# Graph network kernel: the last stages' messages all scattered by GpSimd, none summed by TensorE

## Chip, cores and metric

One NeuronCore of one Trainium2 chip runs the whole program. The metric is the device time of one execution in microseconds; lower is better. Engines: TensorE (PE) multiplies matrices, VectorE (DVE) and ScalarE (ACT) work element by element, GpSimd (POOL) here almost only issues indirect DMAs (gathers and scatters of rows), SyncE (SP) issues the plain DMAs.

## What is computed

A graph of N = 12,500 nodes with D = 16 features and E = 400,000 edges (`src`, `dst`, sorted by `dst`). Four blocks follow each other, each with a residual and a layer norm:

```python
x = layernorm(x + L0(x))   # two graph attention layers
x = layernorm(x + L1(x))   # two graph convolutions
x = layernorm(x + L2(x))   # sheaf: per edge two Householder reflections
x = layernorm(x + L3(x))   # tensor product of node features and edge attributes
# sheaf (L2)
deg = zeros.at[src].add(1).at[dst].add(1)
out = x - zeros.at[src].add(msg_s) - zeros.at[dst].add(msg_d)
# product (L3)
m   = silu(einsum('ei,ej,ijh->eh', x[dst], edge_attr, W) * norm)
agg = segment_sum(m @ W_lin, src)
```

What matters here is the sum of per-edge messages **by source node**. Edges are sorted by destination, so sums by `dst` are scans along the edges; sums by `src` need another way.

## The kernel before

Edge number e = lane * 3125 + column: each of the 128 partitions ("lanes") holds 3,125 consecutive edges. They are worked through in NCH = 25 chunks of CH = 125 columns, and within a chunk in groups of GRP = 5 columns (NG = 25 groups), with two buffers per tile (`b` is 0 or 1).

Two ways to sum by source stand side by side, split by column. The first DC = 20 columns of each chunk (DG = 4 groups) are **direct**: class `DirectSums` (L1310) adds their messages to a PSUM accumulator of all nodes. Per column VectorE makes two one-hot tiles of the source number (L1349, L1351) and their wide product with the message, 128 x 1600 (L1354), and TensorE multiplies that in (four products of 400 columns, L1339). The other SC = 105 columns (SG = 21 groups) are **scattered**: GpSimd writes each column's 128 rows to their places in source order in a DRAM table, one indirect DMA per column (`scatter_column_loop`, L1152). Afterwards `src_order_scan` reads that table in order and scans it, chunk by chunk (16 scans of 105 columns per chunk, L1724), and `extract` picks up the ends.

The place of an edge in source order is its `rank`. It is made along the way: `histograms` counts nodes (beside the first attention gather), `count_in_group` counts equal sources within a group (beside the second attention gather), and `count_before_group` looks up and advances a running table, one group at a time. The last is split over the two graph convolutions: the first (stage names c1...) takes 11 groups of each chunk, the second (c2...) 10.

The order of the work around the change is written by hand, one loop per engine with semaphores between:

- `gcn_gather` (c1 and c2): GpSimd gathers the first 85 columns of each chunk (L494). VectorE and TensorE find the other 40 by matching (`Match`: L1269 makes 13 tiles per step, ten steps a chunk), and each round of VectorE's loop also does one group of `count_before_group` (L1097 to L1108: two one-hot tiles, a lookup tile, a wait for TensorE, a product, a reduction, an add). The loop has as many rounds as the longer of the two: `for m in range(max(NB + 1, side.groups))`, NB + 1 = 11. After it come 16 scans (L975).
- `sheaf_edges` (se...): GpSimd's queue is gather(i+1), scatter(i), gather(i+2), scatter(i+1) and so on: 125 gathers and 105 scatters per chunk. VectorE, TensorE and ScalarE work on chunk i group by group, and the direct columns of chunk i-1 are put between its groups 0 to 19.
- `product_edges` (pe...): GpSimd only scatters, five columns at a time as ScalarE finishes a group (L1851). Per group VectorE makes an outer product (L1787), TensorE transposes (L1815), ScalarE copies (L1849), TensorE multiplies (L1822), ScalarE applies silu. The chunk's own direct columns begin after its first four groups.

```python
for t in range(SC):
    ...
    g.indirect_dma_start(out=view, in_=M[b][:, DC + t, :], in_offset=None,
                         out_offset=bass.IndirectOffsetOnAxis(ap=stage[b][:, t:t + 1], axis=0)
                         ).then_inc(sent[b], 16)
```

## Time and profile before

| | us |
|---|---|
| median of 3 runs | 32684.31 |
| lowest and highest | 32668.05, 32695.04 |
| the profiled execution, its own time | 32672.44 |
| its span, first to last instruction | 32670.6 |
| second attention gather (g2g), first to last gather | 6160.7 to 10135.7 |
| first gcn gather (c1c) | 11322.2 to 14729.9 |
| second gcn gather (c2c) | 15144.2 to 18560.0 |
| sheaf edges, first gather to last scatter | 18959.2 to 27201.0 |
| product edges, first to last scatter | 27984.8 to 32009.8 |

The profile records each instruction of one execution. "Busy" counts the time in an instruction; waits are given by what ended them. A DMA issued by GpSimd is a POOL instruction whose length is the time that POOL spends on issuing it, not the transfer. Line numbers are those of the kernel before.

### The profile page before, as it was taken

Reading aid. Unit: us, or ns where it says so; the run is one execution under the profiler, and the core shown is the slowest. Engines: PE = TensorE matmul, PEld = TensorE weight load, DVE = VectorE, ACT = ScalarE, POOL = GpSimd, SP = SyncE. Lnnn points to the kernel's source line nnn. Section 1 sums busy time; section 2 is a strip of 40 time slices with the busy share of each in tenths; the row PEclk is TensorE's granted clock in tenths of the full one; section 3 lists DMA queues with packets and bytes.
Section 4 is the critical chain, followed back from the end, with each engine's and each line's share of the span. In section 5 each row is a group of like instructions: output and inputs, shape, how many; then the busy total and the mean of one; then the engine's idle time right before and its main releaser. Section 6 shows DMA issues by size and latency. Waiting matters only on the chain. (4 is left out here: it accounts for less than half of the span.)

```text
span 32670.6 us, 266258 instructions
## 1 busy us (share of the span) xinstructions
PE 13491.3 (41%) x71326; PEld 10479.5 (32%) x71326; DVE 16103.5 (49%) x34560; ACT 2584.3 (8%) x3901; POOL 22511.4 (69%) x20275
## 2 busy tenths in 40 slices
PE   1111100211110177775777535444444441666663
PEld 1111100211110166664666423232323230454442
DVE  3434429344443677775777534444444443444442
ACT  0000000000000000000000001011111110333330
POOL 5777760477775288885888767777777774777772
PEclk5555555555555588886888756666666665777775
DMA  2111113111112311111111110000000002000001
GB/s 55 16 15 16 16 10 145 22 27 27 27 27 46 111 33 33 33 32 21 33 33 33 25 15 12 14 12 14 12 14 12 14 10 59 18 15 15 15 13 56
DMA packets 1117655, 946.20 MB, mean 29 GB/s; under 512 B 609084, under 2 KB 1060308, under 8 KB 1092308
## 3 DMA queue, kind: packets, MB, share of 16 engines
q1 hardware_dynamic: 468516, 706.27, 7.3%
q0 software_dynamic: 646368, 201.76, 6.4%
q10 hardware_dynamic: 1872, 28.29, 0.2%
q8 instruction: 307, 5.03, 0.1%
q14 instruction: 592, 4.85, 0.1%
HBM read 506.74 MB, written 428.17 MB: 29 GB/s over the span
## 5 line engine op out<-in xcount | busy, mean ns | idle before, releaser
L494 POOL DMA_INDIRECT g1g_G<-tab,g1g_stage x3125 | 3270.3, 1046 | 1237.8 <-issue 1025.7
L494 POOL DMA_INDIRECT se_G<-tab,se_stage x3125 | 3324.5, 1064 | 1085.3 <-issue 1072.5
L494 POOL DMA_INDIRECT g2g_G<-tab,g2g_stage x3125 | 2949.5, 944 | 1272.5 <-issue 1026.4
L1152 POOL DMA_INDIRECT messages<-pe_M,pe_rstage x2625 | 3178.9, 1211 | 905.3 <-issue 817.5
L1152 POOL DMA_INDIRECT messages<-se_M,se_rstage x2625 | 2980.1, 1135 | 865.7 <-issue 799.6
L494 POOL DMA_INDIRECT c2c_G<-tab16b,c2c_stage x2125 | 2769.4, 1303 | 856.0 <-issue 647.3
L494 POOL DMA_INDIRECT c1c_G<-tab,c1c_stage x2125 | 2761.3, 1299 | 793.7 <-issue 647.3
L1053 DVE SCALAR_TENSOR_TENSOR g2gh_junk<-g2gh_pB,g2gh_src_f,earlier 128x128 f32<-128x128 f32 (+4 forms) x2625 | 1453.7, 614 | 1951.3 <-POOLq L493 1928.0
L1567 PE MATMUL se_pTV<-ident,se_pair 128*32 128x128 f32 x3125 | 539.5, 313 | 4159.9 <-DVE se_pair L1474 4159.4
L739 PE MATMUL g1gh_acc<-g1gh_oh_hi,g1gh_oh_lo 128*128 128x100 bf16 x6250 | 539.0, 283 | 3746.7 <-DVE g1gh_oh_hi L719 3746.7
L1065 PE MATMUL g2gh_pB<-ident_b,src_lo 128*128 128x128 bf16 x2625 | 641.4, 286 | 3290.3 <-DVEq L1059 3249.5
L1278 PE MATMUL c1cm_acc<-c1cm_hot,c1cm_part 128*128 128x512 f32 x6500 | 1740.7, 429 | 344.3 <-DVE c1cm_hot L1269 344.3
L1278 PE MATMUL c2cm_acc<-c2cm_hot,c2cm_part 128*128 128x512 f32 x6500 | 1717.2, 425 | 400.9 <-DVE c2cm_hot L1269 400.9
L1567 PEld LDWEIGHTS se_pTV<-ident,se_pair 128*32 128x32 f32 x3125 | 283.8, 106 | 4534.9 <-issue 4486.2
L739 PEld LDWEIGHTS g1gh_acc<-g1gh_oh_hi,g1gh_oh_lo 128*128 128x128 bf16 x6250 | 508.6, 143 | 3777.1 <-DVE g1gh_oh_hi L719 3777.1
L717 DVE TENSOR_TENSOR g1gh_oh_lo<-dst_lo,iota 128x640 bf16<-128x640 f32 (+1 forms) x625 | 514.6, 823 | 2284.6 <-POOLq L493 2231.8
L1473 DVE COPY se_pair<-se_G 128x80 f32 (+1 forms) x625 | 139.9, 224 | 2888.7 <-DMA se_G<-tab,se_stage 2761.6
L1278 PEld LDWEIGHTS c1cm_acc<-c1cm_hot,c1cm_part 128*128 128x128 f32 x6500 | 1356.2, 213 | 640.7 <-issue 336.7
L1278 PEld LDWEIGHTS c2cm_acc<-c2cm_hot,c2cm_part 128*128 128x128 f32 x6500 | 1338.2, 210 | 691.3 <-issue 389.2
L1787 DVE TENSOR_TENSOR pe_outer<-pe_X,pe_A 128x640 f32 x625 | 520.9, 833 | 1941.8 <-PE pe_pT L1815 1855.5
L1065 PEld LDWEIGHTS g2gh_pB<-ident_b,src_lo 128*128 (+1 forms) x2625 | 278.4, 106 | 3433.3 <-issue 3187.5
L1822 PE MATMUL pe_pM<-p_wm,pe_outT 128*128 128x16 f32 x6250 | 905.2, 283 | 1034.6 <-ACT pe_outT L1849 1034.6
(607 smaller groups left out, 34105.5 us busy)
## 6 DMA issues: line engine op xcount, KB each, us to landing
scans<-g1w_W SPq DMA_DIRECT2D x25, 3187.5 KB, 10.0
c1cm_row<-match SPq DMA_DIRECT2D x500, 128.0 KB, 3.0
c2cm_row<-match SPq DMA_DIRECT2D x500, 128.0 KB, 3.0
edges<-g2g_G SPq DMA_DIRECT2D x25, 2062.5 KB, 6.8
g2w_G<-edges SPq DMA_DIRECT2D x25, 2062.5 KB, 11.6
scans<-g2w_W SPq DMA_DIRECT2D x25, 2062.5 KB, 7.3
g1g_G<-tab,g1g_stage POOLq DMA_INDIRECT x3125, 2.4
g2g_G<-tab,g2g_stage POOLq DMA_INDIRECT x3125
```

The lines of the kernel that those rows point to most:

```text
L494: g.indirect_dma_start(out=G[b][:, t, :], out_offset=None, in_=table, in_offset=bass.IndirectOffsetOnAxis(ap=stage[b][:, t:t + 1], axis=0) ...
L717: v.tensor_tensor(oh_lo[o][b][:, part, :], bc(lo[:, at], [P, m, P], 2), bc(k.iota[:, :], [P, m, P], 1), ALU.is_equal).then_inc(ready, 1)
L739: mm = pe.matmul(acc[2 if o and direct else o][:, 0:NT], oh_lo[o][b][:, g, :], oh_hi[o][b][:, g, :], start=False, stop=True, skip_group_ch ...
L1053: ins = v.scalar_tensor_tensor(out=junk[g][:, :], in0=pB[b][:, a * GRP * P:(e + 1) * P], scalar=src_f[:, e:e + 1], in1=k.earlier[:, (GRP - ...
L1065: pe.matmul(pB[b][:, e * P:(e + 1) * P], k.src_lo[:, at].to_broadcast([P, P]), k.ident_b[:, :], start=True, stop=False)
L1152: g.indirect_dma_start(out=view, in_=M[b][:, DC + t, :], in_offset=None, out_offset=bass.IndirectOffsetOnAxis(ap=stage[b][:, t:t + 1], axis=0)
L1278: mm = pe.matmul(self.acc[m % 2][:, :], self.part[part][:, j * MR:(j + 1) * MR, :].rearrange("p r f -> p (r f)"), self.hot[m % 2][:, j, :] ...
L1473: ch(v.tensor_copy(pair[:, :, 0, :], G[b][:, at, 0:D]))
L1567: mm = pe.transpose(pT[:, g * P:(g + 1) * P], pair[:, g, :, :].rearrange("p n d -> p (n d)"), k.ident[:, :])
L1787: v.tensor_tensor(outer[:, :, :, :], bc(X[b][:, at, :], [P, GRP, D, DE], 3), bc(A[b][:, at, :], [P, GRP, D, DE], 2), ALU.mult).then_inc(ou ...
L1822: mm = pe.matmul(pM[:, g * D:(g + 1) * D], outT[:, g * P:(g + 1) * P], w[:, :], start=True, stop=True)
```

## The change

The direct sums go: class `DirectSums` and all its calls in both stages, the third histogram, and the blocks that add its result. All 125 columns of a chunk are scattered. So the rank is needed for 25 groups instead of 21: `count_in_group` does 25, `count_before_group` 13 in the first graph convolution and 12 in the second. The tables in source order have 3,125 places per lane instead of 2,625, and `src_order_scan` scans 125 columns per chunk.

```diff
@@ -33,11 +33,6 @@
 PAIRS = NCH // 2
 GRP = 5
 NG = CH // GRP
-DG = 4
-DC = DG * GRP
-SG = NG - DG
-SC = SG * GRP
-LS = NCH * SC
 NT = 100
 NP = NT * P
 XT = 25
...
-    steps = [(at, min(size, DC - at), True) for at in range(0, DC, size)] + [(at, min(size, CH - at), False) for at in range(DC, CH, size)]
-    return steps, max(n for _, n, _ in steps)
+    steps = [(at, min(size, CH - at)) for at in range(0, CH, size)]
+    return steps, max(n for _, n in steps)


 def histograms(k, c, name):

...
-    steps = -(-SG // per)
+    steps = -(-NG // per)
     pB = [c.ps(f"{name}_pB{b}", [P, 2048]) for b in range(2)]
     junk = [c.sb(f"{name}_junk{g}", [P, (g + 1) * P]) for g in range(GRP)]
...
@@ -1144,12 +1139,12 @@
 def scatter_column_loop(g, i, j, b, view, M, stage, staged, ready, sent, parts=1):

     g.wait_ge(staged[b], (j + 1) * 16)
-    for t in range(SC):
+    for t in range(CH):
         if parts == 1 and t == 0 or parts > 1 and t % GRP == 0:

-            g.wait_ge(ready, i + 1 if parts == 1 else i * NG + (DG + t // GRP + 1))
+            g.wait_ge(ready, i + 1 if parts == 1 else i * NG + (t // GRP + 1))
             g.nop(nofuse=True)
-        g.indirect_dma_start(out=view, in_=M[b][:, DC + t, :], in_offset=None,
+        g.indirect_dma_start(out=view, in_=M[b][:, t, :], in_offset=None,
                              out_offset=bass.IndirectOffsetOnAxis(ap=stage[b][:, t:t + 1], axis=0)
                              ).then_inc(sent[b], 16)

...
-                s.dma_start(k.rank_lanes.rearrange("p (i c) -> p i c", c=CH)[:, :, DC:CH],
-                            k.rank[:, :].rearrange("p (i c) -> p i c", c=CH)[:, :, DC:CH]).then_inc(stored, 16)
+                s.dma_start(k.rank_lanes, k.rank[:, :]).then_inc(stored, 16)
                 s.wait_ge(stored, 16)

...
@@ -1307,71 +1301,13 @@
                       self.out[:, at:at + BE * D].rearrange("p (e f) -> p e f", f=D)).then_inc(self.emptied, 1)


-class DirectSums:
...
-    def tensor_first(self, pe):
-        pe.wait_ge(self.hot, 4)
-        for b in range(2):
-            self.products(pe, b, b == 0)
-
-    def products(self, pe, b, start):
-        for q in range(self.BANKS):
-            mm = pe.matmul(self.acc[:, q, 0:self.w * D], self.oh_lo[b][:, :],
-                           self.wide[b][:, q * self.w:(q + 1) * self.w, :].rearrange("p t d -> p (t d)"),
-                           start=start, stop=True, skip_group_check=True)
-        mm.then_inc(self.added, 1)
-
-    def vector(self, v, k, M, i, d, b):
-
-        m = i * DC + d
-        at = bass.ds(i * CH + d, 1)
-        v.wait_ge(self.added, m + 1)
-        v.tensor_tensor(self.oh_lo[b][:, :], k.iota[:, :], k.src_lo[:, at].to_broadcast([P, P]),
-                        ALU.is_equal).then_inc(self.made, 1)
-        v.tensor_tensor(self.oh_hi[b][:, :], k.iota[:, 0:NT], k.src_hi[:, at].to_broadcast([P, NT]),
-                        ALU.is_equal).then_inc(self.hot, 1)
-        v.wait_ge(self.hot, m + 5)
-        v.tensor_tensor(self.wide[b][:, :, :], bc(self.oh_hi[b][:, :], [P, NT, D], 2),
-                        M[:, bass.ds(d, 1), 0:D].to_broadcast([P, NT, D]), ALU.mult).then_inc(self.made, 1)
-
-    def tensor(self, pe, i, d, b):
-        pe.wait_ge(self.made, (i * DC + d) * 2 + 2)
-        self.products(pe, b, False)
-
-    def vector_last(self, v, out):
-        v.wait_ge(self.added, NCH * DC + 2)
-        for q in range(self.BANKS):
-            v.tensor_copy(out[:, q * self.w:(q + 1) * self.w, :],
-                          self.acc[:, q, 0:self.w * D].rearrange("p (t d) -> p t d", d=D)).then_inc(self.out_sem, 1)
-
-
 def release_messages(g, b, j, sent, mfree):

-    g.wait_ge(sent[b], (j + 1) * (16 * SC))
+    g.wait_ge(sent[b], (j + 1) * (16 * CH))
...
-                            sums.vector(v, k, M[1 - b], i - 1, d, half)
-
...
-                    spread_column(0, 0)
                     evacuate(0)
-                    with v.Fori(0, DC // 2 - 1) as m:
-                        ch.enter(m, 10)
-                        group_step(2 * m + 1, 1)
-                        group_step(2 * m + 2, 0)
-                        ch.leave(DC // 2 - 1, 10)
-                    group_step(DC - 1, 1)
-                    with v.Fori(DC, NG - 1) as q:
-                        ch.enter(q - DC, 5)
+                    with v.Fori(1, NG - 1) as q:
+                        ch.enter(q - 1, 5)
                         group_step(q)
-                        ch.leave(NG - 1 - DC, 5)
+                        ch.leave(NG - 2, 5)
                     v.wait_ge(evacuated, i * NG + (NG - 1))
                     group_dots(NG - 2)
...
                 with v.Fori(0, PAIRS) as j:
                     ch.enter(j, 2 * per)
-                    chunk(2 * j + 1, 1, j, True)
-                    chunk(2 * j + 2, 0, j + 1, True)
+                    chunk(2 * j + 1, 1, j)
+                    chunk(2 * j + 2, 0, j + 1)
                     ch.leave(PAIRS, 2 * per)
-                v.nop(nofuse=True)
-                with v.Fori(0, DC // 2) as m:
-                    sums.vector(v, k, M[0], NCH - 1, 2 * m, 0)
-                    sums.vector(v, k, M[0], NCH - 1, 2 * m + 1, 1)
-                sums.vector_last(v, direct)

             @block.tensor
             def _(pe):
-                def chunk(i, direct_before):
+                def chunk(i):

                     def transpose(n):
...
-                    with pe.Fori(0, DC // 2) as m:
-                        for half in range(2):
-                            group_step(2 * m + (1 + half), 2 * m + half if direct_before else None, half)
-                    with pe.Fori(DC + 1, NG - 1) as q:
+                    with pe.Fori(1, NG - 1) as q:
                         group_step(q)
                     hidden_layer(i * NG + (NG - 1))
                     pe.wait_ge(evacuated, i * NG + (NG - 1))
                     vectors(i * NG + (NG - 1))
-                sums.tensor_first(pe)
-                chunk(0, False)
-                with pe.Fori(0, PAIRS) as j:
-                    chunk(2 * j + 1, True)
-                    chunk(2 * j + 2, True)
-                with pe.Fori(0, DC // 2) as m:
-                    sums.tensor(pe, NCH - 1, 2 * m, 0)
-                    sums.tensor(pe, NCH - 1, 2 * m + 1, 1)
+                over_chunks(pe, lambda i, b, j: chunk(i))

             @block.scalar
...
@@ -1787,23 +1689,11 @@
                         v.tensor_tensor(outer[:, :, :, :], bc(X[b][:, at, :], [P, GRP, D, DE], 3),
                                         bc(A[b][:, at, :], [P, GRP, D, DE], 2), ALU.mult).then_inc(outered, 1)
                     v.nop(nofuse=True)
-                    with v.Fori(0, DG + 1) as q:
+                    with v.Fori(0, NG) as q:
                         outer_products(q)
-                    v.wait_ge(silued, i * NG + DG)
-                    v.nop(nofuse=True)
-                    with v.Fori(0, DC // 2) as m:
-                        outer_products(2 * m + (DG + 1))
-                        sums.vector(v, k, M[b], i, 2 * m, 0)
-                        outer_products(2 * m + (DG + 2))
-                        sums.vector(v, k, M[b], i, 2 * m + 1, 1)
-                    v.wait_ge(sums.made, (i + 1) * (2 * DC))
                     v.wait_ge(outered, (i + 1) * NG)
-                    v.sem_inc(dfree, 1)
                     v.sem_inc(used, 1)
-                v.sem_inc(dfree, 2)
-                sums.vector_first(v)
                 over_chunks(v, chunk, ch, 2 + D + 1)
-                sums.vector_last(v, direct)

             @block.tensor
...
+                    with pe.Fori(0, NG) as q:
                         transpose(i * NG + q)
                         multiply(i * NG + q)
-
-                    with pe.Fori(0, DC // 2) as m:
-                        for half in range(2):
-                            n = i * NG + 2 * m + (DG + 1 + half)
-                            transpose(n)
-                            sums.tensor(pe, i, 2 * m + half, half)
-                            multiply(n)
-                sums.tensor_first(pe)
                 over_chunks(pe, chunk)

             @block.scalar
             def _(a):
                 def chunk(i, b, j):
...
@@ -2174,16 +2055,16 @@
                 ch(v.tensor_tensor(agg[:, :, :], agg[:, :, :], bc(dinv[:, :], [P, NT, D], 2), ALU.mult))
             vector_block(k, name + "f", finish)

-        half = SG // 2 + 1
+        half = NG // 2 + 1
         aggregate("c1", k.x[:, :, :], tab16, lambda k, c, n: count_before_group(
-            k, c, n, DG, half, k.by_src["start"]))
+            k, c, n, 0, half, k.by_src["start"]))
         with ExitStack() as s2:
             h = Ctx(nc, s2).sb("c_h", [P, NT, HG])
             node_linear(k, "ch", agg, w1[:, :], h, D, HG)
             batch_norm_relu(k, "cn", h, b1, gamma, beta, HG)
             node_linear(k, "co", h, w2[:, :], y, HG, D)
         aggregate("c2", y[:, :, :], tab16b, lambda k, c, n: count_before_group(
-            k, c, n, DG + half, SG - half, k.free_place))
+            k, c, n, half, NG - half, k.free_place))

         def residual(v, ch):
             ch(v.tensor_tensor(y[:, :, :], agg[:, :, :], bc(b2[:, :], [P, NT, D], 1), ALU.add))
...
         vector_block(k, "sd", degrees)
         root_inverse(k, "sr", xd[:, :, D], xd[:, :, D], 1e-5)
         store_nodes(k, "st", [xd[:, :, :]], tab)
```

Two places where the instruction streams differ, as they stand in program order. `ISA` rows are waits and no-ops, `REGISTER_ALU` rows compute addresses and counts. First VectorE at the end of a chunk of the first gcn stage (`c1ch_...` are the tiles of `count_before_group`, `c1cm_...` those of the matching). Before:

```order
L1102 TENSOR_SCALAR c1ch_loT<-c1ch_pB,part 128x640
L1105 TENSOR_TENSOR c1ch_prod<-c1ch_pR,c1ch_oh_hi 128x500
L75 REGISTER_ALU
L1107 TENSOR_REDUCE c1ch_r<-c1ch_prod 128x5
L75 REGISTER_ALU
L1108 ISA
L1108 TENSOR_TENSOR rank<-c1ch_r,rank 128x5
L1306 COPY c1c_G<-c1cm_out 128x64
L972 ISA
L973 REGISTER_ALU
L975 ISA
L975 SCALAR_TENSOR_TENSOR c1c_G<-keep_d,carry,c1c_G 128x125 x16
```

The eleventh round's group, the last copy of matched columns, then the scans. In the changed kernel two more groups stand between that copy and the scans. The first begins so:

```order
L1103 TENSOR_TENSOR rank<-c1ch_r,rank 128x5
L1300 COPY c1c_G<-c1cm_out 128x64
L1091 REGISTER_ALU
L1092 ISA
L1092 TENSOR_TENSOR c1ch_oh_lo<-src_lo,iota 128x640
L1094 REGISTER_ALU
L1094 TENSOR_TENSOR c1ch_oh_hi<-src_hi,iota 128x500
```

and the second ends so:

```order
L1100 TENSOR_TENSOR c1ch_prod<-c1ch_pR,c1ch_oh_hi 128x500
L70 REGISTER_ALU
L1102 TENSOR_REDUCE c1ch_r<-c1ch_prod 128x5
L70 REGISTER_ALU
L1103 ISA
L1103 TENSOR_TENSOR rank<-c1ch_r,rank 128x5
L967 ISA
L968 REGISTER_ALU
L970 REGISTER_ALU
L970 SCALAR_TENSOR_TENSOR c1c_G<-keep_d,carry,c1c_G 128x125 x16
```

These two groups have no matching step beside them. The second place is VectorE in the product stage, from the sixth group of a chunk on. Before:

```order
L1794 ISA
L1787 ISA
L1787 REGISTER_ALU
L1787 TENSOR_TENSOR pe_outer<-pe_X,pe_A 128x640
L1348 ISA
L1349 ISA
L1349 TENSOR_TENSOR ped_ohl<-iota,src_lo 128x128
L1351 REGISTER_ALU
L1351 TENSOR_TENSOR ped_ohh<-iota,src_hi 128x100
L1353 REGISTER_ALU
L1354 ISA
L1354 TENSOR_TENSOR y<-ped_ohh,pe_M 128x1600
```

After each outer product (L1787) the one-hot tiles and the wide product of a direct column follow. In the changed kernel the loop over the groups has the outer product alone, and the next chunk follows:

```order
L1692 UNCONDITIONAL_BRANCH
L1692 ISA
L1689 ISA
L1689 REGISTER_ALU
L1689 TENSOR_TENSOR pe_outer<-pe_X,pe_A 128x640
L1692 REGISTER_ALU
L1692 COMPARE_AND_BRANCH
L1694 ISA
L1682 ISA
L1682 TENSOR_SCALAR pe_begin<-keep_d 128x125
```

On GpSimd the order is the same, with 125 in place of 105 scatters in a row.

## Rows read from the trace of the kernel before

**Rows 1.** the page: busy time by engine, and POOL in 40 slices

```profile
PE 13491.3 (41%) x71326; PEld 10479.5 (32%) x71326; DVE 16103.5 (49%) x34560; ACT 2584.3 (8%) x3901; POOL 22511.4 (69%) x20275
...
POOL 5777760477775288885888767777777774777772
```

**Rows 2.** groups by line: xcount | busy us, mean ns | idle before, its releasers

```profile
L494 POOL DMA_INDIRECT se_G<-tab,se_stage x3125 | 3324.5, 1064 | 1085.3 <-issue 1072.5 <-DMA se_stage<-in_src_dram 12.8
...
L1152 POOL DMA_INDIRECT messages<-pe_M,pe_rstage x2625 | 3178.9, 1211 | 905.3 <-issue 817.5 <-ACT pe_M L1851 64.8 <-DMA messages<-pe_M,pe_rstage 23.0
L1152 POOL DMA_INDIRECT messages<-se_M,se_rstage x2625 | 2980.1, 1135 | 865.7 <-issue 799.6 <-DVE se_M L1533 66.1
L494 POOL DMA_INDIRECT g2g_G<-tab,g2g_stage x3125 | 2949.5, 944 | 1272.5 <-issue 1026.4 <-DMA g2g_stage<-in_src_dram 246.1
...
L1349 DVE TENSOR_TENSOR sed_ohl<-iota,src_lo 128x128 f32<-128x128 f32 x500 | 146.3, 293 | 125.4 <-DVE se_dots L1487 116.4 <-PE sed_acc L1339 8.4 <-DVE carry L1544 0.5
```

**Rows 3.** waits: engine line <- what ended them: us in total, times, longest us

```profile
DVE se_pair L1473 <- DMA se_G<-tab,se_stage: 2761.6, 24, 150.3
...
DVE g2gh_junk L1053 <- POOLq L493: 1928.0, 398, 21.6
...
ACT L1849 <- POOLq L1371: 509.6, 10, 53.2
...
POOL messages L1152 <- ACT pe_M L1851: 64.8, 17, 58.2
```

**Rows 4.** instructions by tile, carry: ns min/median/max, first and last start us

```profile
L978 DVE COPY carry<-c1c_G x25: 174/176/383, 11467.5 to 14778.6; 128x16 f32<-128x16 f32 x25
L978 DVE COPY carry<-c2c_G x25: 174/175/386, 15294.6 to 18568.4; 128x16 f32<-128x16 f32 x25
...
  DMA c2c_G<-tab16b,c2c_stage: 119.3, 24
...
  DMA c1c_G<-tab,c1c_stage: 6.4, 1
```

**Rows 5.** instructions by tile, se_M: ns min/median/max, first and last start us

```profile
L1152 POOL DMA_INDIRECT messages<-se_M,se_rstage x2625: 954/959/2592, 19313.7 to 27201.0; - x188
```

**Rows 6.** timeline, sheaf stage, 20404 to 20407: start us, us, engine, line

```profile
20403.70 1.83 DVE L1354 TENSOR_TENSOR s_agg<-sed_ohh,se_M 128x1600 f32<-128x1600 f32 x1 [0.16 <-DVE sed_ohh L1351]
...
20404.50 1.86 POOL L1152 DMA_INDIRECT messages<-se_M,se_rstage  x1 [0.30 <-issue]
```

**Rows 7.** busy by window: us, PE, PEld, DVE, ACT, POOL busy (x), PEclk, DMA

```profile
19140.00:19260.00 120.00, 105.92 (x341) 70.73 (x341) 31.20 (x123) 26.74 (x36) 90.75 (x97) 0.50 0.10 7
19500.00:19560.00 60.00, 0.00 (x0) 0.00 (x0) 52.00 (x62) 0.00 (x0) 49.03 (x37) 0.50 0.17 42
19680.00:19780.00 100.00, 97.67 (x441) 64.28 (x439) 65.33 (x161) 23.74 (x34) 79.47 (x68) 0.95 0.05 6
```

**Rows 8.** timeline, product stage, 28107 to 28109

```profile
28107.43 0.83 DVE L1787 TENSOR_TENSOR pe_outer<-pe_X,pe_A 128x640 f32 x1 [3.43 <-PE pe_pT L1815]
28107.67 1.42 POOL L1152 DMA_INDIRECT messages<-pe_M,pe_rstage  x1 [0.30 <-issue]
```

**Rows 9.** timeline, first gcn stage, VectorE at the end of a chunk

```profile
12142.36 0.68 DVE L1105 TENSOR_TENSOR c1ch_prod<-c1ch_pR,c1ch_oh_hi 128x500 f32<-128x500 f32 x1 [4.57 <-PE c1ch_pR L1127]
...
12144.91 0.84 DVE L1097 TENSOR_TENSOR c1ch_oh_lo<-src_lo,iota 128x640 bf16<-128x640 f32 x1
...
12149.81 0.68 DVE L1105 TENSOR_TENSOR c1ch_prod<-c1ch_pR,c1ch_oh_hi 128x500 f32<-128x500 f32 x1 [2.54 <-PE c1ch_pR L1127]
...
12151.53 0.22 DVE L1306 COPY c1c_G<-c1cm_out 128x64 f32<-128x64 f32 x1
12151.88 6.03 DVE L975 TENSOR_TENSOR_SCAN c1c_G<-keep_d,carry,c1c_G 128x125 f32<-128x125 f32 x16
```

**Rows 10.** timeline, second gcn stage, VectorE in the last round of a chunk

```profile
16381.16 0.23 DVE L1306 COPY c2c_G<-c2cm_out 128x64 f32<-128x64 f32 x1 [1.16 <-PE c2cm_out L1298]
```

**Rows 11.** timeline, product stage's scan, one chunk

```profile
32068.91 5.36 DVE L1724 TENSOR_TENSOR_SCAN ps_O<-keep_s,carry,ps_G 128x105 f32<-128x105 f32 x16
```

More of the change, by code:

```diff
@@ L708, in vector @@
     def vector(v, ch, i, q, b, landed):
-        start, n, _ = steps[q]
+        start, n = steps[q]
         v.wait_ge(used, i * len(steps) + q + 1)
@@ L734, in tensor @@
     def tensor(pe, i, q, b):
-        start, n, direct = steps[q]
+        _, n = steps[q]
         pe.wait_ge(ready, i * made[-1] + made[q])
@@ L1368, in release_messages, with sheaf_edges @@
 def release_messages(g, b, j, sent, mfree):
-    g.wait_ge(sent[b], (j + 1) * (16 * SC))
+    g.wait_ge(sent[b], (j + 1) * (16 * CH))
     g.nop(nofuse=True).then_inc(mfree[b], 1)
-def sheaf_edges(k, name, table, scans, messages, first, carry, w1, b1, w2, b2, direct, wide):
+def sheaf_edges(k, name, table, scans, messages, first, carry, w1, b1, w2, b2):
     F = D + 1
@@ L1400, in sheaf_edges @@
         pH = c.ps(name + "_pH", [P, 2, 512])
-        sums = DirectSums(c, name + "d", wide)
         staged = [c.sem(f"{name}_staged{b}") for b in range(2)]
@@ L1731, in _, with product_edges @@
                     v.tensor_reduce(k.whole[:, :], k.keep_s[:, :], axis=AX.X, op=ALU.min).then_inc(whole, 1)
-def product_edges(k, name, attr, messages, first, w, direct, wide):
+def product_edges(k, name, attr, messages, first, w):
     with ExitStack() as st:
@@ L1746, in product_edges @@
         pM = c.ps(name + "_pM", [P, 512])
-        sums = DirectSums(c, name + "d", wide)
         rstaged = [c.sem(f"{name}_rstaged{b}") for b in range(2)]
@@ L2291, in residual @@
             ch(v.tensor_tensor(y[:, :, :], y[:, :, :], agg[:, :, :], ALU.add))
-            ch(v.tensor_tensor(y[:, :, :], y[:, :, :], direct[:, :, :], ALU.add))
             ch(v.tensor_tensor(y[:, :, :], y[:, :, :], bc(xd[:, :, D], [P, NT, D], 2), ALU.mult))
@@ L2312, in product @@
         agg = c.sb("p_agg", [P, NT, D])
-        direct = c.sb("p_direct", [P, NT, D])
         load_small(k, "pl", [
@@ L2320, in product @@
         spread(k, "pp", k.x, D, tab, first[:, 0:D])
-        product_edges(k, "pe", attr, messages, first, wm, direct, (y, agg))
+        product_edges(k, "pe", attr, messages, first, wm)
         src_order_scan(k, "ps", messages, scan16, carry, D, False)
@@ L2324, in product @@
         extract(k, "px", scan16, k.by_src, y, D, ALU.add)
-        vector_block(k, "pj", lambda v, ch: ch(v.tensor_tensor(y[:, :, :], y[:, :, :], direct[:, :, :], ALU.add)))
         node_linear(k, "pn", y, wl[:, :], agg, D, D)
```

111 lines of the change are left out of this document (42 added, 69 removed).

## The prediction

> **What bounds the kernel now.** I start with the page: POOL is the busiest engine, 69% of the span and 5 to 8 tenths in nearly every slice, and the stages where it is not are short [rows 1]. The groups by line say with what: indirect DMAs, each about 1 us busy with 0.3 us of "issue" ahead of it, and almost nothing waited for [rows 2]. In the sheaf stage 5,750 of them take 3324.5 + 1085.3 + 2980.1 + 865.7 = 8256 us, which is the length of the stage (18959.2 to 27201.0). In the product stage 2,625 take 3178.9 + 905.3 = 4084 us, again the stage. So both are bound by POOL's queue. The waits show the others idle behind it: VectorE waits 2761.6 us for gathered rows in the sheaf stage (115 us per chunk), ScalarE 509.6 us for POOL to free a buffer in the product stage, VectorE 1928 us for POOL in the second attention gather [rows 3].
>
> The two gcn stages are different. In c1 VectorE ends a chunk every (14778.6 - 11467.5) / 24 = 137.96 us and waits for gathers once, 6.4 us; POOL's last gather starts at 14729.9, 49 us ahead of VectorE's end. There VectorE's own chain sets the pace. In c2 the period is (18568.4 - 15294.6) / 24 = 136.4 us and VectorE waits 119.3 us in all, 4.8 us per chunk: POOL sets it, with VectorE close behind [rows 4].
>
> **The change part by part.**
>
> *1. 500 more scatters in each stage.* The median scatter is 0.959 us busy [rows 5], with 0.305 us before it (799.6 / 2623, [rows 2]): 1.264 us. 500 of them are 632 us per stage, all on the path, +1264 us.
>
> *2. The direct sums go.* TensorE's products, the one-hot tiles and 1,000 wide products leave engines that wait for POOL, so by themselves they give nothing. But they also act on POOL. A scatter issued while a wide product of 1.83 us runs takes 1.86 us instead of 0.96, ending 0.83 us after the product does [rows 6]. How much per wide product? In the sheaf stage gathers are 3324.5 - 3125 x 0.944 = 374 us over the undisturbed length (0.944 is the mean of g2g, where none is disturbed), scatters 2980.1 - 2625 x 0.959 = 463 us [rows 2, 5], 837 us together. The tail of a chunk, with its long operations of 2,000 elements, stays: 37 gathers have 49.03 us there, 14.1 us over [rows 7], 353 us in 25 chunks. Beside short group operations with no wide product (first window, chunk 0) 97 gathers take 90.75 us, nothing over. So the 500 wide products hold 837 - 353 = 484 us, 0.97 us each; the third window, with wide products among the groups, has 68 scatters with 14.3 us over in 100 us. In the product stage 3178.9 - 2625 x 0.959 = 661 us are over. An outer product of 0.83 us makes a scatter 1.42 us, 0.46 us over [rows 8], 625 times 288 us, and they stay; with some 12 us for the chunk starts, 361 us are left for 500 wide products, 0.72 us each. Given back: 484 + 361 = 845 us. Bounds from rows for a wide product: 0 (POOL would be held elsewhere anyway) and its whole 1.83 us.
>
> Here a rule speaks for another size. By the Trainium skill (SBUF — State Buffer, "Who interferes with whom") a tensor_tensor takes only the read interface of the port pair shared with GpSimd, while writing descriptors needs the write interface, so it would not stall them (the skill calls that inferred). By that rule this part would give 0 us. The trace disagrees with it, 1.86 us against 0.96 us.
>
> *3. Four more groups in count_before_group, 13 and 12 per chunk.* In c1 they stand alone between the matching and the scans. The nearest row is the eleventh group, also with no multiply beside it: from its first tile at 12144.91 to the copy behind it at 12151.53 it takes 6.62 us, 2.54 of them waiting for TensorE [rows 9]. 2 x 6.62 us per chunk on the engine that sets the pace: 25 x 13.24 - 6.4 (the one wait) = +325 us. In c2 one group falls into a round that so far waited 1.16 us for TensorE [rows 10], so I take 5.4 us, and one stands alone, 6.6 us: 25 x 12.0 - 119.3 = +181 us; VectorE takes the pace over from POOL. Bounds for a group: 4.1 us (no wait for TensorE) and 8.6 us (the wait of 4.57 us of the round before [rows 9], whose products queue behind a match). I take 6.62, the row with the same neighbours.
>
> *4. Four more groups in count_in_group.* VectorE waits 1928 us for POOL there [rows 3], and POOL's gathers stay at 0.944 us beside this work [rows 2]: nothing. The work is 1/5 more of some 1,800 us and is covered by that wait; without it, it would cost about 340 us.
>
> *5. Scans in source order.* 16 scans of 105 columns take 5.36 us [rows 11], 16 of 125 take 6.03 us [rows 9]; VectorE sets the pace in both: 2 x 25 x 0.67 = +34 us.
>
> *6. Ends and starts.* In the product stage POOL's first scatter waits up to 58.2 us for a message [rows 3], because four groups pass before the first scattered column; now the first group's columns go at once: -28 us. The wait at the start of the sheaf stage stays, chunk 0 had no direct sums. Clearing the wide tiles, emptying the accumulators, adding the results: -10 us. The histograms have the same seven steps.
>
> What becomes late next? Without direct sums TensorE does less, and its granted clock will be lower. Chunk 0 of the sheaf stage shows that case: 0.50 of full speed, that is 1.2 GHz, for the groups [rows 7]. Its 125 gathers of 1.247 us end near 19115 and its first scatter starts at 19313.7 [rows 5], so such a chunk takes some 199 us and has over 300 us of POOL's queue to lie behind. In the product stage a group without direct sums takes 0.83 + 3.43 = 4.3 us [rows 8] against 6.8 us for its five scatters (5 x 1.264 + 0.46). Both stay bound by POOL.
>
> **Sum:** 1264 - 845 + 325 + 181 + 34 - 28 - 10 = +921 us. Against the profiled execution's 32672.4 us that is 33593 us; the median shown lies 12 us above that execution, so 33605, rounded **33600 us**, 2.8% slower. A measurement of this kernel tells about 0.2% (65 us) from no change.
>
> **The rivals.**
>
> *A. The wide products' hold on POOL was not theirs.* POOL would be as long per scatter without them, because another operation would take their place. (That is the time that the skill's rule would give.) For it: the short VectorE operations of the groups also read two tiles and disturb nothing [rows 7]. Against it: the single rows, and that the excess stands only where long operations run. Then the 845 us do not come back: 32684 + 921 + 845 = 34450 us. Chance 0.05.
>
> *B. The added gcn groups are hidden.* If POOL sets the pace in both gcn stages they cost nothing: 33600 - 506 = 33094 us. For it: POOL's period is within 2 us of VectorE's in c1. Against it: then VectorE would wait for gathers in c1, and it does not [rows 4]; hiding 12 or 13 us needs that much idle time, and there are 4.8 in c2. Chance 0.04.
>
> *C. Faster: each direct column costs POOL the length of all its VectorE work.* The mechanism is the lock-out of POOL by VectorE in the sheaf and product stages, at a price above what the lengths show. All other terms add 1264 + 506 + 34 - 38 = 1766 us, so from 1.77 us per direct column on the change wins. If POOL were held for the wide product and the one-hot tile of 0.29 us [rows 2] ahead of it, 2.12 us, the time would be 32684 + 1766 - 2120 = 32330 us. Against it: 1,000 such holds are 2,120 us, and POOL's excess in both stages is 837 + 661 = 1,498 us in all, 641 of which belong to operations that stay. Chance 0.02.
>
> **How the numbers follow.** My forecast has 0.89. Its own spread: groups that never wait for TensorE give -190 us (75 of them), groups of 8.6 us +150 us; a wide product in the product stage as dear as in the sheaf stage -125 us; POOL's outer products holding longer once scatters are denser, or 0.2 us less given back per wide product, +200 us. Not all at once: **33370 to 33830 us**, which leaves A, B and C outside, 0.11. Every case but C is slower by far more than 0.2%: slower 0.97, same 0.01, faster 0.02.
>
> **What the profile after would show.** 3,125 scatters per stage, medians still 0.96 us, means down from 1.135 to about 1.07 us in the sheaf stage and from 1.211 to about 1.06 us in the product stage; no scatter of 1.86 us among a chunk's groups, the 2 us ones at its tail still there. A VectorE period of about 151 us in c1 and 144 us in c2, and POOL waiting for buffers there for the first time. Stage lengths: sheaf 8,400 us, product 4,300 us between first and last scatter. The attention stages unchanged to a few us. I am wrong if the means do not fall (A), if the gcn periods stay near 137 us (B), or if VectorE's or ScalarE's wait for POOL vanishes in the last two stages, which would mean a slower chain per group than I took.

## The result and the profile after

The changed kernel takes **33710.63 us** (median of 4 runs, 33709.77 to 33728.73) where the kernel before took 32686.44 us beside it: a ratio of 1.0315, 95% interval [1.0298, 1.0333], 1024 us slower. The forecast was 33600 us, range 33370 to 33830: slower as predicted, 111 us more than the point. The profiled execution after took 33711.01 us, its span 33709.2 us.

The page of the changed kernel, as [rows 1]:

```profile
PE 13340.5 (40%) x66293; PEld 10813.0 (32%) x66293; DVE 14582.4 (43%) x33290; ACT 2640.1 (8%) x4001; POOL 22595.5 (67%) x21275
...
POOL 5777751577772587756887577777777774777772
PEclk5555555555555687877777655555555555555555
```

POOL is still the busiest engine. It issues 1,000 more indirect DMAs and is busy only 84 us more than before. The groups by line, as [rows 2]:

```profile
L489 POOL DMA_INDIRECT se_G<-tab,se_stage x3125 | 3329.6, 1065 | 1085.3 <-issue 1072.3
L1147 POOL DMA_INDIRECT messages<-pe_M,pe_rstage x3125 | 3219.7, 1030 | 1126.3 <-issue 1039.5
...
L1147 POOL DMA_INDIRECT messages<-se_M,se_rstage x3125 | 3010.8, 963 | 1086.4 <-issue 1019.4
L489 POOL DMA_INDIRECT c1c_G<-tab,c1c_stage x2125 | 2758.7, 1298 | 998.4 <-issue 642.8
L489 POOL DMA_INDIRECT c2c_G<-tab16b,c2c_stage x2125 | 2779.3, 1308 | 905.2 <-issue 645.4
```

The scatters' means fell from 1135 to 963 ns and from 1211 to 1030 ns: over the undisturbed 0.959 us they are now 3010.8 - 2996.9 = 14 us in the sheaf stage (463 before) and 223 us in the product stage (661 before). The sheaf's gathers did not change, 1065 ns against 1064. But the idle time ahead of the scatters rose by 221 us in each stage, where 500 gaps of 0.305 us are 152. The carry copies, one at the end of each chunk of the gcn stages, give the length of a chunk (the period). As [rows 4] (instructions by line: ns min/median/max, first and last start us):

```profile
L973 DVE COPY carry<-c1c_G x25: 174/175/176, 11478.1 to 15093.8; 128x16 f32<-128x16 f32 x25
L973 DVE COPY carry<-c2c_G x25: 174/174/177, 15607.4 to 19075.1; 128x16 f32<-128x16 f32 x25
```

The periods are 150.7 us in c1 and 144.5 us in c2 (138.0 and 136.4 before). The table sets the stages of the two traces side by side, from starts of POOL's first and last indirect DMA and of the last carries; its last column sums to the 1038.6 us between the spans.

| stretch | predicted | measured |
|---|---|---|
| start to c1's first gather (both attention stages) | 0 | +4.9 |
| to c1's last carry | +325 | +310.3 |
| to c2's last carry | +181 | +191.5 |
| to the sheaf's first gather | -10 | -7.7 |
| to the sheaf's last scatter | +632 - 484 = +148 | +256.5 |
| to the first product scatter (scans +17, start -28) | -11 | -14.0 |
| to the last product scatter | +632 - 361 = +271 | +286.6 |
| to the end (scans) | +17 | +10.5 |

So nearly the whole net miss is in the sheaf stage, 108 us of it. The larger part of these is a wait that I had passed over; it stands in the product stage as well, where other errors hide it, as told behind the experiments. POOL's timeline in the changed product stage:

```profile
28873.30 0.95 POOL L1147 DMA_INDIRECT messages<-pe_M,pe_rstage  x1 [0.30 <-issue]
28877.24 0.95 POOL L1147 DMA_INDIRECT messages<-pe_M,pe_rstage  x1 [2.99 <-issue]
28878.50 0.96 POOL L1147 DMA_INDIRECT messages<-pe_M,pe_rstage  x1 [0.31 <-ACT pe_M L1732]
```

Ahead of the 114th scatter of a chunk POOL idles 2.99 us instead of 0.30, and nothing in the profile releases it. This happens in each of the 25 chunks of both stages of the changed kernel. It was in the trace before as well, 3.25 us ahead of the 114th gather in each chunk of the attention stages and of the sheaf stage, but never in a block of 105 scatters or of 85 gathers. The change makes blocks of 105 into blocks of 125 and so buys the pause twice: 2 x 25 x 2.68 = 134 us.

### The profile page after: what moved, and what is told of

Its sections match the earlier page's. It is cut to its first block and busy times, and to the rows that moved or that the text cites. A ratio compares the mean times of both kernels' runs of the same rounds, so it can differ in the third digit from the quotient of the medians.

```text
span 33709.2 us, 256675 instructions
## 1 busy us (share of the span) xinstructions
PE 13340.5 (40%) x66293; PEld 10813.0 (32%) x66293; DVE 14582.4 (43%) x33290; ACT 2640.1 (8%) x4001; POOL 22595.5 (67%) x21275
## 5 line engine op out<-in xcount | busy, mean ns | idle before, releaser
L489 POOL DMA_INDIRECT se_G<-tab,se_stage x3125 | 3329.6, 1065 | 1085.3 <-issue 1072.3
L1147 POOL DMA_INDIRECT messages<-pe_M,pe_rstage x3125 | 3219.7, 1030 | 1126.3 <-issue 1039.5
L1147 POOL DMA_INDIRECT messages<-se_M,se_rstage x3125 | 3010.8, 963 | 1086.4 <-issue 1019.4
L1481 PE MATMUL se_pTV<-ident,se_pair 128*32 128x128 f32 x3125 | 780.0, 416 | 4465.8 <-DVE se_pair L1408 4465.8
L1048 DVE SCALAR_TENSOR_TENSOR g2gh_junk<-g2gh_pB,g2gh_src_f,earlier 128x128 f32<-128x128 f32 (+4 forms) x3125 | 1731.0, 614 | 1659.3 <-POOLq L488 1622.9
L1712 PE MATMUL pe_pM<-p_wm,pe_outT 128*128 128x16 f32 x6250 | 1446.0, 376 | 1857.2 <-ACT pe_outT L1730 1857.2
L1712 PEld LDWEIGHTS pe_pM<-p_wm,pe_outT 128*128 128x128 f32 x6250 | 1378.8, 329 | 2108.0 <-ACT pe_outT L1730 2108.0
L1060 PE MATMUL g2gh_pB<-ident_b,src_lo 128*128 128x128 bf16 x3125 | 758.1, 281 | 3189.4 <-DVEq L1054 3147.8
L1481 PEld LDWEIGHTS se_pTV<-ident,se_pair 128*32 128x32 f32 x3125 | 361.9, 133 | 5104.9 <-issue 4986.3
L1495 PE MATMUL se_pTV<-s_w,se_hid 128*128 128x32 f32 x6250 | 1464.8, 404 | 493.3 <-ACT se_pairT L1516 468.9
L1495 PEld LDWEIGHTS se_pTV<-s_w,se_hid 128*128 128x128 f32 x6250 | 1381.5, 330 | 804.7 <-ACT se_pairT L1516 757.7
L1488 PE MATMUL se_pH<-se_pairT,s_w 32*128 32x320 f32 x2500 | 1561.4, 777 | 19.6 <-ACT se_pairT L1516 19.6
```

The costliest lines, as they stand in the source:

```text
L489: g.indirect_dma_start(out=G[b][:, t, :], out_offset=None, in_=table, in_offset=bass.IndirectOffsetOnAxis(ap=stage[b][:, t:t + 1], axis=0) ...
L1048: ins = v.scalar_tensor_tensor(out=junk[g][:, :], in0=pB[b][:, a * GRP * P:(e + 1) * P], scalar=src_f[:, e:e + 1], in1=k.earlier[:, (GRP - ...
L1060: pe.matmul(pB[b][:, e * P:(e + 1) * P], k.src_lo[:, at].to_broadcast([P, P]), k.ident_b[:, :], start=True, stop=False)
L1147: g.indirect_dma_start(out=view, in_=M[b][:, t, :], in_offset=None, out_offset=bass.IndirectOffsetOnAxis(ap=stage[b][:, t:t + 1], axis=0)) ...
L1481: mm = pe.transpose(pT[:, g * P:(g + 1) * P], pair[:, g, :, :].rearrange("p n d -> p (n d)"), k.ident[:, :])
L1488: mm = pe.matmul(pH[:, h, 0:HALF], w1[:, :], pairT[:, h, :], start=True, stop=True)
```

## The experiments

A run has the number of its label: run 8 is e8.

**1. Whose is the hold on POOL?** In the kernel before the wide product is cut to 16 elements; it leaves out 99 of the 100 tiles of the direct sums.

```
-  v.tensor_tensor(self.wide[b][:, :, :], bc(self.oh_hi[b][:, :], [P, NT, D], 2),
-                  M[:, bass.ds(d, 1), 0:D].to_broadcast([P, NT, D]), ...
+  v.tensor_tensor(self.wide[b][:, 0:1, :], bc(self.oh_hi[b][:, 0:1], [P, 1, D], 2),
+                  M[:, bass.ds(d, 1), 0:D].to_broadcast([P, 1, D]), ...
```

> The kernel before, in which VectorE's wide product of a direct column is 16 elements in place of 1,600 (everything else of the direct sums stays: one-hot tiles, TensorE's four products, waits). It leaves out all but the first of the 100 tiles of the direct sums. Theory H (the wide product holds POOL for about 0.9 us each while it runs): scatters of the sheaf stage fall from 1135 to about 965 ns mean (2980 to about 2531 us), of the product stage from 1211 to about 1044 ns (3179 to about 2741 us), gathers of the sheaf stage stay at 1064 ns; the time falls by about 449 + 438 = 887 us to about 31800 us. Rival (the hold is not the wide product's, something else of the chunk takes its place, or the whole of the direct sums is what costs): means stay within 3% and the time stays within 100 us of 32684 us. A price over 1.77 us per direct column would show as a gain over 1770 us.

31847.68 us, ratio 0.9738 [0.9721, 0.9754]: 850 us less than the kernel before beside it, where 887 were expected.

```profile
L1152 POOL DMA_INDIRECT messages<-pe_M,pe_rstage x2625 | 2730.3, 1040 | 904.9 <-issue 807.8
L1152 POOL DMA_INDIRECT messages<-se_M,se_rstage x2625 | 2549.3, 971 | 884.0 <-issue 799.6
```

The scatters lost 431 us of busy time in the sheaf and 449 us in the product stage, 0.86 and 0.90 us per wide product. TensorE's four products per column, the one-hot tiles and the waits were still there. What the scatters still have over 0.959 us is 32 us in the sheaf stage, where the changed kernel, without any of these, has 14, and 213 us in the product stage, where it has 223. So the hold belongs to the wide product, all but 18 us of it at most. Rival A falls, and so does rival C, which needed over 1.77 us per column.

**2. What in the wide product holds POOL?** The kernel before, with the one-hot row of the product stage in PSUM.

```
-  self.oh_hi = [c.sb(f"{name}_ohh{b}", [P, NT]) for b in range(2)]
+  self.oh_hi = [... if hot is None else hot[:, b * NT:(b + 1) * NT] for b in range(2)]
...
+  hot = c.ps(name + "_hotps", [P, 512])
-  sums = DirectSums(c, name + "d", wide)
+  sums = DirectSums(c, name + "d", wide, hot)
```

> The kernel before, in which the one-hot row of the product stage's direct sums (the first input of the wide product) lies in PSUM in place of SBUF; same elements, same order, sheaf stage untouched. Theory H2 (POOL is held because the wide product takes two inputs from SBUF): the product stage's scatters fall from 1211 to about 1044 ns mean and the time by about 440 us to about 32245 us. Rival R2 (it is held by any VectorE operation of that length, by its writes for instance): the mean stays at 1211 ns and the time at 32684 us, or some us more if reading PSUM is slower. The sheaf stage's scatters stay at 1135 ns by both.

32246.82 us, ratio 0.9862 [0.9846, 0.9879]. The timeline of the product stage shows it (start us, us, engine, line):

```profile
29040.84 1.82 DVE L1354 TENSOR_TENSOR p_agg<-pe_hotps,pe_M 128x1600 f32<-128x1600 f32 x1
29041.44 0.96 POOL L1152 DMA_INDIRECT messages<-pe_M,pe_rstage  x1 [0.30 <-issue]
```

The same rows of the kernel before, with both inputs in SBUF:

```profile
29068.27 1.83 DVE L1354 TENSOR_TENSOR p_agg<-ped_ohh,pe_M 128x1600 f32<-128x1600 f32 x1
29068.88 2.05 POOL L1152 DMA_INDIRECT messages<-pe_M,pe_rstage  x1 [0.31 <-issue]
```

VectorE takes as long, 1.82 us, and writes the same 1,600 elements to SBUF, but a scatter issued 0.6 us into it takes 0.96 us instead of 2.05. The group's mean fell to 1040 ns, exactly as with the tiny product, while the sheaf stage's, unedited, stayed at 1132. The hold goes with the second input from SBUF, not with the length of the product or its output. The Trainium skill (SBUF — State Buffer, "Who interferes with whom") has a rule that fits, that a VectorE instruction with two SBUF inputs contends with a GpSimd instruction that reads SBUF; its inference two bullets further, that a tensor_tensor does not stall descriptor generation, does not fit these rows: 2.05 us against 0.96 us for POOL's indirect DMA.

**3. One input, many operations.** The kernel before, with the sheaf stage's wide product made by 16 tensor_scalar operations.

```
+  v.tensor_copy(self.row[b][:, :], M[:, bass.ds(d, 1), 0:D].rearrange("p a d -> p (a d)")) ...
+  for f in range(D):
+      v.tensor_scalar(self.wide[b][:, :, f], self.oh_hi[b][:, :], self.row[b][:, f:f + 1], None, ALU.mult)
```

> The kernel before, in which the sheaf stage's wide product is made by 16 tensor_scalar operations of 100 elements (the one-hot row times one value of the message, a scalar of each lane), each with one tensor from SBUF, in place of one tensor_tensor with two. Product stage untouched. Theory H2 (two inputs from SBUF hold POOL): sheaf scatters fall from 1135 to about 970 ns mean as they did with the tiny product, the sheaf stage by about 440 us, the time to about 32250 us; VectorE gets some 2 to 4 us more per direct column, up to 80 us per chunk, and has 115 us per chunk to lie in. Rival R3 (any VectorE work that lasts that long holds POOL, or tensor_scalar takes a faster mode that holds it as well): the mean stays near 1135 ns or rises, the time stays at 32684 us or goes over it. The product stage stays at 1211 ns by both.

That run and runs 6 and 7 fell on a chip on which the kernel before itself took 39207.45 us, so that their times say nothing against the others: 40029.9 us for this one (ratio 1.0227), 39511.36 us (ratio 1.0069) and 42014.71 us (1.0722) for the two below. There the sheaf stage is not POOL's: its scatters waited 3020.4 us for VectorE's messages in the sixth run. All three were run again elsewhere.

> The kernel of the fifth run once more; the chip of runs five to seven ran the kernel before itself in 39207 us, 20% over what it took on the first chip, with VectorE, not POOL, setting the pace of the sheaf stage, so they can't tell the theories apart by time. On a chip where the kernel before takes its 32690 us: by theory H2 (two inputs from SBUF hold POOL) sheaf scatters fall from 1135 to about 970 ns and the time to about 32250 us; by rival R3 (tensor_scalar holds POOL as well) the mean stays near 1135 ns or more and the time at 32684 us or over. On the slow chip the mean of the sheaf scatters was 1053 ns against 1120 ns with the wide tensor_tensor, half of the way.

32455.0 us, ratio 0.9926 [0.9909, 0.9942].

```profile
L1152 POOL DMA_INDIRECT messages<-se_M,se_rstage x2625 | 2734.8, 1042 | 872.0 <-issue 799.6 <-DVE se_M L1541 72.4
```

A miss for both theories as sized: the scatters lost 245 us of the 431 that they could. Between the 2549 us without the wide product and these 2735 us lie 0.37 us per column, spread over 3.1 us of VectorE's work. In the trace some 190 us of what the scatters have over 0.959 us stand on those that overlap most with these operations. So 16 operations with one tensor input from SBUF still hold POOL some of the time; why is open.

**4. What is the pause ahead of the 114th?** The changed kernel; sheaf stage: columns 65 to 124 scattered before 0 to 64; product stage: two semaphores.

```
+  order = [*range(65, CH), *range(65)] if parts == 1 else [*range(CH)]
...
-                       ).then_inc(sent[b], 16)
+                       ).then_inc(sent2[b] if sent2 and t >= 65 else sent[b], 16)
```

> The changed kernel with two edits that ask why POOL idles some 3.0 us before the 114th scatter of each chunk. Sheaf stage: the columns of a chunk are scattered in another order, columns 65 to 124 first, then 0 to 64. Product stage: the first 65 columns signal one semaphore, the last 60 another. Theory C (it counts indirect DMAs that follow each other with one semaphore): in the sheaf stage the gap stays before the 114th, in the product stage it is gone, 25 x 2.7 = 68 us less, 33643 us. Theory D (it belongs to the column, its addresses): in the sheaf stage the gap moves to the 49th scatter (column 113), in the product stage it stays. Theory E (it belongs to the place in the program, a straight run of over 113 indirect DMAs): both stay where they are before the 114th and the time stays at 33711 us.

33646.74 us, 64 us less than the changed kernel.

```profile
L1148 POOL DMA_INDIRECT messages<-pe_M,pe_rstage x3125 | 3221.8, 1031 | 1060.4 <-issue 992.6 <-ACT pe_M L1737 67.7
L1148 POOL DMA_INDIRECT messages<-se_M,se_rstage x3125 | 3011.4, 964 | 1086.6 <-issue 1019.5 <-DVE se_M L1455 67.2
```

In the sheaf stage the 25 pauses of 3.0 us stayed ahead of the 114th, whatever column that is; in the product stage they went, idle time down by 66 us. That is theory C: D (the column) fails in the sheaf stage, E (the place in the program) in the product stage. The pause comes with more than 113 indirect DMAs of one block on one semaphore. Blocks of 85 and 105 that come back to the same semaphore chunk after chunk have none, so the count starts again with each block; whether the other block's semaphore or the waits between restart it was not tested. The same for gathers, with the edit of run 2 (columns 65 and on signal got2[b], and VectorE waits for both semaphores):

> The kernel before with two edits: the product stage's one-hot row in PSUM as in the second run, and the gathers of the first and second attention stage and of the sheaf stage with two semaphores per chunk, 65 columns and 60. Theory C (a pause of 3.2 us before the 114th indirect DMA in a row on one semaphore): the three gathers' pauses go, 3 x 25 x 2.93 = 220 us less if POOL sets the pace in all three, so 32247 - 220 = 32027 us, and their idle time falls from 1238, 1273 and 1085 us by 73 us each. Rival (the pause is hidden in the attention stages, where others wait for other things too): only the sheaf's 73 us, 32170 us.

> The kernel of the sixth run once more, for the same reason. In the sixth run no gather had a pause before the 114th of a chunk, where the fifth run had 25 of 3.2 us in the first attention gather: theory C held for gathers in its mechanism. Its price on a chip of the first kind: 3 x 73 = 220 us, 32027 us; by the rival (hidden in the attention stages) 32170 us.

32106.53 us, ratio 0.9819 [0.9803, 0.9835], some 145 us beyond run 2 (each against the kernel before beside it), between the two expectations of 220 and 73 us.

```profile
L494 POOL DMA_INDIRECT se_G<-tab,se_stage x3125 | 3329.3, 1065 | 1032.4 <-issue 1019.5 <-DMA se_stage<-in_src_dram 12.9
L494 POOL DMA_INDIRECT g1g_G<-tab,g1g_stage x3125 | 3290.1, 1053 | 1163.1 <-issue 952.0 <-DMA g1g_stage<-in_src_dram 211.1
...
L494 POOL DMA_INDIRECT g2g_G<-tab,g2g_stage x3125 | 2949.2, 944 | 1198.6 <-issue 951.9 <-DMA g2g_stage<-in_src_dram 246.7
```

All pauses went: 3125 gaps of 0.305 us are the 952 us of the attention stages. Against [rows 2] g2g gained 74 us. In g1g the gathers took 20 us more, and in the sheaf stage only 53 us of idle time went: POOL's wait after every second block of scatters, for these to land and for the next round of its loop to begin, went from 4.8 to 6.8 us, in 10 rounds. Why it is longer is open.

**5. What is a gcn group worth?** The changed kernel with the 25 groups split 11 and 14, and 15 and 10, in place of 13 and 12 (`half = 11`, `half = 15`).

> The changed kernel with the 25 groups of count_before_group split 11 to c1 and 14 to c2 in place of 13 and 12. Theory G (each added group adds its own length on VectorE, which sets the pace): c1's period returns from 150.6 to 138.0 us, the stage is 315 us shorter; c2 gets two groups of 6.6 us, 25 x 13.2 = +330 us, its period goes from 144.5 to about 157.7 us; in all +15 us, 33725 us. Rival G2 (part of the added time is POOL's, the stages are close to its pace, so a group is dearer in one stage than in the other): c1's period does not return to 138 us, or c2's rises by clearly less or more than 13.2 us, and the total moves by over 60 us.

> The changed kernel with the 25 groups of count_before_group split 15 to c1 and 10 to c2 in place of 13 and 12. Theory G (a group costs its length on VectorE where VectorE sets the pace, and less the idle time where it does not): c2 returns to the period of 136.4 us and the 3274 us between its first and last carry of before, 194 us less; c1 gets two more groups of 6.6 to 7.2 us, 330 to 360 us; in all +140 to +170 us, 33850 to 33880 us. Rival (the c2 stage of the changed kernel is longer for another reason, the scatters' state or the clock): c2's period stays above 138 us.

> The kernel of the seventh run once more, for the same reason. Theory G: c2's period back at 136.4 us (194 us less than in the changed kernel), c1 two more groups of 6.6 to 7.2 us, +330 to +360 us, 33850 to 33880 us in all. Rival: c2's period stays above 138 us.

33766.34 us (11 and 14) and 33886.88 us (15 and 10), against 33725 us and 33850 to 33880 us expected. The carries of the one and of the other:

```profile
L973 DVE COPY carry<-c1c_G x25: 174/175/375, 11468.6 to 14767.3; 128x16 f32<-128x16 f32 x25
L973 DVE COPY carry<-c2c_G x25: 174/175/176, 15290.5 to 19102.5; 128x16 f32<-128x16 f32 x25
```

```profile
L973 DVE COPY carry<-c1c_G x25: 174/175/176, 11489.7 to 15432.7; 128x16 f32<-128x16 f32 x25
L973 DVE COPY carry<-c2c_G x25: 174/175/384, 15944.7 to 19262.5; 128x16 f32<-128x16 f32 x25
```

c1's periods with 11, 13 and 15 groups are 137.4, 150.7 and 164.3 us: 6.6 and 6.8 us a group, a straight line. c2's with 10, 12 and 14 groups are 138.2, 144.5 and 158.8 us: 3.1 us a group up to 12, where POOL's pace hides part, then 7.2. With its old number of groups c2 stands 1.8 us per chunk above the 136.4 of the kernel before, so the expected return to 136.4 failed by 44 us in the stage, and the rival's sign, over 138 us, came; POOL's gathers are longer there, 2808.8 us against 2769.4 before. That is close to what one trace differs from another (2739 to 2817 us in the runs of this section), but part may be real.

**6. Together.** The kernel before with the edits of runs 2, 8 and 9; and the changed kernel with two semaphores in all five blocks of 125.

> The kernel before with all three edits: the product stage's one-hot row in PSUM, the sheaf stage's wide product as 16 tensor_scalar operations, two semaphores for the 125 gathers of a chunk. If the gains add (451 us in the second run, 247 in the eighth, 145 in the ninth beyond the second): 32690 - 843 = about 31850 us, ratio 0.974. If the sheaf stage's VectorE becomes the pace once POOL is faster, less: VectorE still waited for gathered rows by some 100 us per chunk in the eighth run, so I expect the gains to add within 40 us.

> The changed kernel with two semaphores for the 125 columns of a chunk in all five blocks of 125 indirect DMAs (gathers of both attention stages and of the sheaf stage, scatters of the sheaf and the product stage). Theory C: the pause before the 114th goes from all; the gathers give 145 us as they did in the kernel before, the product stage's scatters 64 us as in the fourth run, the sheaf stage's scatters 25 x 2.7 = 67 us at most: 33711 - 276 = 33435 us. Rival (in the sheaf stage the order of the block, not the semaphore, decides): the sheaf scatters keep 25 pauses of 3.0 us and the time is 33500 us.

31902.28 us, ratio 0.9751 [0.9735, 0.9767], and 33419.9 us, ratio 1.0220 [1.0203, 1.0237]. The gains add up to 806 us against the kernel before beside it, 37 short of the sum. The sheaf's scatters are what is short: 2785.4 us there against 2734.8 in run 8, with the same 16 operations beside them; why they hold more in this run is open.

```profile
L1154 POOL DMA_INDIRECT messages<-se_M,se_rstage x2625 | 2785.4, 1061 | 881.7 <-issue 799.6 <-DVE se_M L1545 82.1
```

The second kernel was expected at 33435 us. In it the sheaf's scatters have no pause left:

```profile
L1149 POOL DMA_INDIRECT messages<-se_M,se_rstage x3125 | 3010.9, 963 | 1025.1 <-issue 952.3 <-DVE se_M L1459 72.8
```

With the pauses gone from both forms and most of the hold gone from the first, the direct sums are worth 1518 us, not 1024. The first of the two is the fastest kernel of this study that does the whole work; run 1, 55 us below it, leaves most of the direct sums out.

## Why the prediction was right, and where it was off

**The frame held.** POOL's queue sets the sheaf and product stages, and each scatter costs its 1.264 us there; what TensorE and VectorE no longer do gives nothing except through POOL. The waits of the changed kernel (engine, line, what ended them: us in total, times, longest us), as [rows 3]:

```profile
DVE se_pair L1407 <- DMA se_G<-tab,se_stage: 2761.5, 24, 150.3
...
DVE g2gh_junk L1048 <- POOLq L488: 1622.9, 423, 19.3
```

VectorE waits as long as before for gathered rows in the sheaf stage, to 0.1 us (2761.5 against 2761.6 [rows 3]), although the granted clock fell to 0.50 in all slices of the last stages, the lower of the two levels, as forecast, and a matmul of pe_pM went from 283 to 376 ns. ScalarE's wait for POOL to free a buffer in the product stage did not vanish either: 870 us before, 905 us after.

But in the product stage the margin was thinner than I took. I read a group's 4.3 us off a chunk of odd number [rows 8]. In the 12 even chunks from 0 to 22 ScalarE loads its function table twice per group, 1.28 us each, before and after the change, and a group of the changed kernel takes 6.03 us there, where five undisturbed scatters take 5 x 1.264 = 6.3 us (a row by source line, a row of the timeline):

```profile
L1730 ACT ACT_TABLE_LOAD  x300: 1283/1283/1283, 28703.4 to 32505.6; - x150
30009.58 0.82 DVE L1689 TENSOR_TENSOR pe_outer<-pe_X,pe_A 128x640 f32 x1 [5.19 <-PE pe_pT L1705]
```

POOL stayed the slower one, but not by the 2.5 us per group that I had.

**Step 2, the hold, was right in kind, wrong in its parts.** 449 + 438 = 887 us came back where I had 484 + 361 = 845. That the sum is off by only 42 us is luck: one part was 35 us too high, the other 77 too low. In the sheaf stage I mixed gathers and scatters. The gathers' excess (374 us) did not move, so none of it was the wide products'; the scatters' excess of 463 us was nearly all the wide products'. Kept apart, the scatters' 463 us would have been 3% over the 449. In the product stage I priced an outer product by one row, 0.46 us [rows 8], and 12 us for the chunk starts. After the change 223 us are left over: 171 us stand on the scatters that overlap most with an outer product, 0.27 us for each, and 55 us on those beside the operations at a chunk's start. Run 2 leaves much the same, 211 us.

**The step that failed is 1, the price of the added scatters.** I took median plus mean gap of 105 scatters and multiplied by 500, as if a block of 125 were a block of 105 and 20 more. The pause ahead of the 114th adds 68 us to the sheaf and 67 us to the product stage. It stood in the rows I had: g2g's issue time of 1026.4 us over 3,125 gathers is 0.328 us, against 0.305 us for the sheaf's scatters [rows 2], though single gaps read 0.30 us in both. The difference of 0.023 us is one pause of 3 us in 125.

Sheaf: 632 - 449 + 68 + 5 (gathers) = 256 us, measured 256.5. Product: 632 - 438 + 67 = 261 us, and 24 waits at a chunk's first message that went from 2.27 to 3.37 us in the mean, 26 us: 287 us, measured 286.6. So the forecast of 271 us for this stage was close by luck: a pause of 67 us and waits of 26 us that it did not have against 77 us more given back.

The longer waits are not spread over the chunks. The chunks inside a round of POOL's loop, which takes two chunks, wait 2.1 us before and after; the 11 that open a new round went from 2.5 to some 4.8 us. Runs with blocks of 105 show a mean of 2.28 us, those with 125 show 3.4 us, two semaphores or one. So it comes with the longer round, 250 scatters in place of 210; what it is stays open.

**Step 3, the gcn groups.** 325 and 181 us were predicted, 310 and 192 us measured, and experiment 5 gives the 6.6 us of c1 directly. POOL now waits for buffers there, as forecast, 209 us in c1 and 51 us in c2. Rival B falls: hidden groups would have left c1 at 138 us. **Step 4** held: g2g's gathers are at 944 ns, and VectorE's wait for POOL there shrank from 1928.0 to 1622.9 us and covered the work. **Steps 5 and 6**: the scans and the starts came within 10 us each.

**The means I said to look for** were off the same way: 1.07 us in the sheaf stage put the whole tail on the scatters, and 963 ns says that it lies over the gathers. In the product stage 1.06 us stands against 1.030.

## What to carry to other kernels

Price an instruction that is added to a block by blocks of the new length, not of the old, and look at the idle time ahead of it by its place in the block: a mean gap hides a pause that comes once per block. Split an engine's excess by group before giving it to a cause, since what is over on gathers and what is over on scatters came from different operations here. And before removing work because it holds another engine, ask what in it does: here one operand moved to PSUM gave back 451 us for one more PSUM tile, and removing the work lost 1024.

## What the runs showed of the hardware

- A tensor_tensor of 1.83 us with both inputs in SBUF holds an indirect DMA that POOL issues while it runs (2.05 us instead of 0.96). With one of the inputs in PSUM and the output still in SBUF it does not (0.96 us).
- 16 tensor_scalar operations with one tensor input from SBUF, 3.1 us in all, still cost POOL 0.37 us per column in run 8 and, by the same reckoning, 0.47 us in run 11.
- POOL pauses 3.0 to 3.3 us (medians) ahead of the 114th indirect DMA of a block on one semaphore, in gathers and scatters alike, with waits for other semaphores in between or without. A second semaphore from the 66th on takes the pause away; blocks of 105 and 85 have none.
- On one chip the kernel before took 39207 us instead of 32690. In the trace of run 6, taken there, POOL waited 3020.4 us in the sheaf stage for VectorE's messages, and VectorE's L1055 still took 613 ns (614 ns in run 9, the same kernel on a faster chip). A comparison across chips would have read as 20%.
